# Expert tiles that wait for single chunks, slots filled from the front, and the first gathers moved into the experts' stage

## What is computed

```python
logits = xf @ Wg + bg
topv, topi = jax.lax.top_k(logits, K)              # K = 2
wts = jax.nn.softmax(topv, axis=-1)
order = jnp.argsort(-wts[:, 0])
...
cap = int(CAP_RATIO * T / E)                       # 1.25 * T / 8 = 15680
oneh = jax.nn.one_hot(tiF, E, dtype=jnp.int32)     # tiF: the picks in that order
pos = jnp.take_along_axis(jnp.cumsum(oneh, axis=0) - 1, tiF[:, None], axis=1)[:, 0]
keep = pos < cap
...
h = jax.nn.gelu(jnp.einsum('ecd,edf->ecf', eb, W1) + b1[:, None, :], approximate=False)
y = jnp.einsum('ecf,efd->ecd', h, W2) + b2[:, None, :]
contrib = yf[slot] * gate[:, None]
```

## Time and profile before

| | us |
|---|---|
| median of 3 runs | 6634.87 (6634.27 to 6637.27) |
| the profiled execution | 6633.88 |
| its span, first to last instruction | 6632.1 |

### The profile page before, as it was taken

The page is one execution under the profiler, slowest core; times in us unless marked ns, Lnnn a source line. Parts: engine busy times, 40 slices in busy tenths (PEclk is TensorE's granted clock), DMA queues, the critical chain, the costliest instruction groups (busy, mean ns, idle before and its releaser), DMA issues. The chain is left out here.

```text
span 6632.1 us, 69063 instructions
## 1 busy us (share of the span) xinstructions
PE 4831.6 (73%) x20564; PEld 2709.5 (41%) x20564; DVE 2371.6 (36%) x4527; ACT 1459.2 (22%) x3608; POOL 3834.9 (58%) x3737
## 2 busy tenths in 40 slices
PE   9999996102777979877987783466776677777778
PEld 4555666101444444434544441233333333333334
DVE  0012248970222222212222222444445545444442
ACT  2233344500222323222332230000000010000001
POOL 0000000008887888778877825777777777777770
PEclk9999998555888989888998896688888888888889
DMA  8877779812333333232333223222222222222210
GB/s 170 185 185 196 192 201 275 286 56 65 100 98 103 108 97 89 86 86 85 101 89 87 74 58 106 81 87 91 89 88 76 70 72 71 93 76 76 76 39 29
DMA packets 840381, 711.46 MB, mean 107 GB/s; under 512 B 596030, under 2 KB 681668, under 8 KB 836048
## 3 DMA queue, kind: packets, MB, share of 16 engines
q1 hardware_dynamic: 666320, 466.30, 25.8%
q0 software_dynamic: 109312, 139.69, 7.8%
q10 hardware_dynamic: 64512, 102.79, 4.5%
HBM read 440.11 MB, written 385.75 MB: 125 GB/s over the span
## 5 line engine op out<-in xcount | busy, mean ns | idle before, releaser
L1077 POOL DMA_INDIRECT y_ring<-ye,index_o x1568 | 1675.3, 1068 | 539.9 <-issue 452.1
L758 POOL DMA_INDIRECT xe<-chunk,index x1568 | 1539.6, 982 | 477.4 <-issue 476.1
L1110 PE MATMUL cp<-padded,taps_o 128*128 128x448 f32 x4032 | 1623.5, 561 | 49.8 <-DVE padded L1296 49.8
L1110 PEld LDWEIGHTS cp<-padded,taps_o 128*128 128x128 f32 x4032 | 785.5, 198 | 816.2 <-issue 795.6
L887 ACT ACTIVATE hid<-hid_ps,b_cols 128x448 f32<-128x448 f32 x1120 | 709.4, 633 | 1663.2 <-PE hid_ps L841 1565.1
L849 PE MATMUL y_ps<-hid,w_sb 128*128 128x448 f32 x2240 | 918.5, 554 | 0.4 <-DVE yt L912 0.4
L841 PE MATMUL hid_ps<-xt,w_sb 128*128 128x448 f32 x2240 | 890.9, 541 | 1.5 <-DVE xt L906 1.5
L1241 DVE SCALAR_TENSOR_TENSOR z<-y_ring,gates,z 128x128 f32<-128x128 f32 x1568 | 432.0, 347 | 905.0 <-DMA y_ring<-ye,index_o 890.1
L470 POOL MEMSET zeros<- 98x512 f32 x1 | 0.5, 524 | 1109.7 <-POOLq L105 1109.7
L1174 ACT ACTIVATE outb<-cp,shift,s 128x448 f32<-128x448 f32 x224 | 162.1, 723 | 2175.0 <-PE cp L1110 2175.0
L906 DVE COPY xt<-xt_ps 128x448 f32<-128x448 f32 x280 | 174.9, 625 | 1280.8 <-PE xt_ps L832 1278.2
(11 more groups left out here) (190 smaller groups left out, 3862.1 us busy)
## 6 DMA issues: line engine op xcount, KB each, us to landing
xe<-zeros SPq DMA_DIRECT2D x16, 3920.0 KB
rows_in<-xe SPq DMA_DIRECT2D x280, 224.0 KB, 2.6
ye<-rows_out SPq DMA_DIRECT2D x280, 224.0 KB, 2.3
xin<-in_x_dram SPq DMA_DIRECT2D x256, 196.0 KB
conv<-rows ACTq DMA_DIRECT2D x256, 196.0 KB
pix<-conv SPq DMA_DIRECT2D x224, 224.0 KB, 5.1
xn<-hat SPq DMA_DIRECT2D x112, 448.0 KB, 4.4
chunk<-xn POOLq DMA_DIRECT2D x112, 448.0 KB, 3.9
```

What stands on the lines that cost most here:

```text
L758: pool.indirect_dma_start(out=xe[:, :], out_offset=bass.IndirectOffsetOnAxis(ap=index[ch][:, c, j:j + 1], axis=0), in_=chunk[ch][:, j * C: ...
L1077: pool.indirect_dma_start(out=y[ch][c][:, j * C:(j + 1) * C], out_offset=None, in_=ye[:, :], in_offset=bass.IndirectOffsetOnAxis(ap=index[ ...
L1110: last = pe.matmul(cp[i % 2][:, 0:HB * W], taps[:, t, :], padded[b][:, img, hb * HB + kh:hb * HB + kh + HB, kw:kw + W], start=(t == 0), st ...
```

## The change

- Slots fill from the front: `spare` is gone. A token's slot starts from its expert's first slot, and an expert with fewer rows than its capacity leaves its last slots empty.
- `needed` counts chunks (1 to 112), not pairs. It is worked out with one tile per partition and brought into a row by a small DMA of SP.
- POOL waits after each chunk until that chunk's own scatters have landed, and raises `chunks_scattered`. The waits for the scatters of earlier chunks go.
- `y_ring`, its semaphores and the index tiles are allocated outside the two last stages. When the scatter is done, POOL copies the indices and clears the ring's parts for the first 4 chunks (`PRE`), waits until the first 14 rounds of tiles are stored (no row of the first pair of images can lie behind them, as the slots fill from the front), and gathers the 4 chunks. The output stage starts with the fifth.
- SP also writes zeros over each expert's slots 6272 to 15679 of `ye` (8 transfers), in the route stage.
- The convolution's weights pass through `summed[1]` in place of the last part of `y_ring`; its first load of x waits until they are read.
- The bound of the indirect DMAs' indices is put into a register once per stage instead of being given as a number with each DMA.

```diff
+PRE = 4
@@ route_phase
+    LATE = 2 * HW
+    ZL = (CAP - LATE) // ZP
...
+            for e in range(E):
+                sp.dma_start(ye[e * CAP + LATE:(e + 1) * CAP, :].rearrange("(p a r) c -> p a (r c)", p=ZP, r=4),
+                             zeros[:].unsqueeze(1).to_broadcast([ZP, ZL // 4, 4 * C])).then_inc(zeroed, 16)
+            sp.wait_ge(needed_set, 1)
+            sp.dma_start(needed[0:1, :, :], needed_by_tile[0:TILES, :]).then_inc(needed_out, 16)
+            sp.wait_ge(needed_out, 16)
+            sp.wait_ge(zeroed, 16 * (ZD + E))
...
+            pe.matmul(sums[:, 0, 0:1], below[:], tile_rows[:], start=True, stop=True).then_inc(tiles_counted, 1)
...
+            do(dve.tensor_tensor(tile_end[:], sums[:, 0, 0:1], tile_rows[:], ALU.add))
...
             scan_flags(work[:], 1)
-            do(dve.tensor_scalar(spare[:], run[:, :, GR - 1], -1.0, float(CAP), ALU.mult, ALU.add))
-            do(dve.tensor_tensor(run, run, spare[:].unsqueeze(2).to_broadcast([128, E, GR]), ALU.add))
-            do(dve.tensor_tensor(spare[:], spare[:], expert_base[:], ALU.add))
-            do(dve.tensor_tensor(base, base, spare[:].unsqueeze(2).to_broadcast([128, E, GR]), ALU.add))
+            do(dve.tensor_tensor(base, base, expert_base[:].unsqueeze(2).to_broadcast([128, E, GR]), ALU.add))
+            do(dve.tensor_scalar(short[:], run[:, :, 0:GR - 1], tile_end[:, 0:1], None, ALU.is_lt))
+            do(dve.tensor_reduce(fewer[:], short[:], AX_X, ALU.add))
+            dve.tensor_scalar(needed_by_tile[:], fewer[:], 1.0, None, ALU.add).then_inc(needed_set, 1)
             do(dve.tensor_tensor(groups_flat(tokens_flat(prio)), before_token, over_tokens(base), ALU.add))
-            do(dve.tensor_tensor_scan(tile_end[:], one_row[:, 0:1].to_broadcast([128, TILES]),
-                                      tile_rows[:, 0:1].to_broadcast([128, TILES]), 0.0, ALU.mult, ALU.add))
-            by_pair = run.rearrange("p e (g c) -> p e g c", c=NCHK)[:, :, 0:PR - 1, NCHK - 1]
-            do(dve.tensor_tensor(short[:], by_pair.unsqueeze(1).to_broadcast([128, TILES, E, PR - 1]),
-                                 tile_end[:].unsqueeze(2).unsqueeze(3).to_broadcast([128, TILES, E, PR - 1]), ALU.is_lt))
-            do(dve.tensor_reduce(fewer[:], short[:], AX_X, ALU.add))
-            do(dve.tensor_scalar(needed[:], fewer[:], 1.0, None, ALU.add))
@@ expert_phase
+    FIRST_PAIR = 2 * HW // NT
...
+            limit = pool.to_reg(DROP - 1)
...
-                    if not (first and ch < 2):
-                        pool.wait_ge(scattered[ahead], ahead_pair * PER_PAIR)
-                    if not first or ch == NCHK - 1:
-                        pool.wait_ge(scattered[(ch + 1) % NCHK], (g + (ch + 1) // NCHK) * PER_PAIR)
...
-                                bounds_check=DROP - 1, oob_is_err=False).then_inc(scattered[ch], 16)
+                                bounds_check=limit, oob_is_err=False).then_inc(scattered[ch], 16)
                     rest(n)
-                    if ch == 0 and not first:
-                        for c in range(NCHK):
-                            pool.wait_ge(scattered[c], g * PER_PAIR)
-                        pool.sem_inc(pairs_scattered, 1)
+                    pool.wait_ge(scattered[ch], (g + 1) * PER_PAIR)
+                    pool.sem_inc(chunks_scattered, 1)
...
+            for ch in range(PRE):
+                pool.tensor_tensor(index_o[ch][:], slots[:, :, ch * CHK:(ch + 1) * CHK],
+                                   zero[:].unsqueeze(2).to_broadcast([128, 2, CHK]), ALU.add).then_inc(index_set, 1)
+                pool.memset(y_ring[:, ch * 2 * CC:(ch + 1) * 2 * CC], 0.0).then_inc(index_set, 1)
+            pool.wait_ge(index_set, PR * NCHK + 1 + 2 * PRE)
+            for i in range(RING):
+                pool.wait_ge(tile_out[i], 16 * FIRST_PAIR * E // RING)
+            for ch in range(PRE):
+                for j in range(CHK):
+                    for c in range(2):
+                        pool.indirect_dma_start(
+                            out=y_ring[:, (ch * 2 + c) * CC + j * C:(ch * 2 + c) * CC + (j + 1) * C], out_offset=None, in_=ye[:, :],
...
-                sp.wait_ge(pairs_scattered, sp.value_load(needed[0:1, bass.ds(q, 1), e:e + 1].rearrange("p q e -> p (q e)"),
-                                                          min_val=1, max_val=PR))
+                sp.wait_ge(chunks_scattered, sp.value_load(needed[0:1, bass.ds(q, 1), e:e + 1].rearrange("p q e -> p (q e)"),
+                                                           min_val=1, max_val=PR * NCHK))
@@ output_phase
-        wc_rows = y_ring[:, (NCHK - 1) * 2 * CC:(NCHK - 1) * 2 * CC + C * 9]
+        wc_rows = summed[1][:, 0:C * 9]
...
             load_x(0, 0)
+            sp.wait_ge(const_turned, 10)
             load_x(1, 1)
...
-            set_index(0, 0)
+            set_index(PRE, PRE)
             def pair(g, first):
-                for ch in range(NCHK):
+                for ch in range(PRE if first else 0, NCHK):
```

More of the change, by code:

```diff
@@ L394, in _, with route_phase @@
                 chunk(m)
-def route_phase(nc, s, logits, xe, slots, gates, needed):
+def route_phase(nc, s, logits, xe, ye, slots, gates, needed):
     PR, J, CAP, DROP, TILES = s["PR"], s["J"], s["CAP"], s["DROP"], s["TILES"]
@@ L406, in route_phase @@
     ZP, ZR, ZD = 98, 80, 16
-    assert ZP * ZR * ZD == E * CAP
+    LATE = 2 * HW
+    ZL = (CAP - LATE) // ZP
+    assert ZP * ZR * ZD == E * CAP and ZP * ZL == CAP - LATE and ZL % 4 == 0
     GR = PR * NCHK
@@ L428, in route_phase @@
         taken = junk
-        expert_base, spare = sb("expert_base", [128, E]), sb("spare", [128, E])
-        tile_rows, tile_end = sb("tile_rows", [128, 1]), sb("tile_end", [128, TILES])
-        short, fewer = sb("short", [128, TILES, E, PR - 1], BF16), sb("fewer", [128, TILES, E])
+        expert_base = sb("expert_base", [128, E])
+        tile_rows, tile_end = sb("tile_rows", [128, 1]), sb("tile_end", [128, 1])
+        short, fewer, needed_by_tile = sb("short", [128, E, GR - 1], BF16), sb("fewer", [128, E]), sb("needed_by_tile", [128, E], U32)
         total = ctx.enter_context(nc.psum_tensor("total", [128, GROUPS, 512], F32))
@@ L654, in _, with expert_phase @@
                 do(dve.tensor_scalar(slots[:, c, 0:J], rel[:], float(DROP), None, ALU.add))
-def expert_phase(nc, s, xn, xe, ye, slots, needed, ln_beta, W1, b1, W2, b2, layer_scale):
+def expert_phase(nc, s, xn, xe, ye, slots, needed, index_o, y_ring, y_in, ln_beta, W1, b1, W2, b2, layer_scale):
     PR, DROP, TM, CAP, TILES = s["PR"], s["DROP"], s["TM"], s["CAP"], s["TILES"]
@@ L667, in expert_phase @@
     PER_PAIR = 2 * CHK * 16
+    FIRST_PAIR = 2 * HW // NT
+    assert FIRST_PAIR * NT == 2 * HW and RING == E
     with ExitStack() as ctx:
@@ L936, in _, with output_phase @@
             result(end - 1, E - 1, TILES - 1, False)
-def output_phase(nc, s, x, xn, ye, ln_beta, slots, gates, out, p):
+def output_phase(nc, s, x, xn, ye, ln_beta, slots, gates, index, y_ring, y_in, out, p):
     PR, N = s["PR"], s["N"]
@@ L968, in output_phase @@
         cleared = sem("cleared")
-        index = [sb(f"index_o{c}", [128, 2, CHK], U32) for c in range(NCHK)]
-        y_ring = sb("y_ring", [128, NCHK * 2 * CC])
         y = [[y_ring[:, (c * 2 + i) * CC:(c * 2 + i + 1) * CC] for i in range(2)] for c in range(NCHK)]
-        wc_rows = y_ring[:, (NCHK - 1) * 2 * CC:(NCHK - 1) * 2 * CC + C * 9]
         z = [sb(f"z{c}", [128, CC]) for c in range(NCHK)]
         summed = [sb(f"summed{b}", [C, 2 * HW]) for b in range(2)]
+        wc_rows = summed[1][:, 0:C * 9]
         padded = [sb(f"padded{b}", [C, 2, H + 2, PW]) for b in range(2)]
@@ L989, in output_phase @@
         index_set = sem("index_o_set")
-        y_in = [sem(f"y_in{c}") for c in range(NCHK)]
         xn_in = [sem(f"xn_in{c}") for c in range(NCHK)]
@@ L1052, in _ @@
             pool.wait_ge(zero_set, 1)
+            limit = pool.to_reg(s["DROP"] - 1)
             def set_index(n, slot):
@@ L1070, in pair @@
                     set_index(n + 1, (ch + 1) % NCHK)
-                    if first and ch == NCHK - 1:
-                        pool.wait_ge(const_turned, 10)
                     pool.memset(y_ring[:, ch * 2 * CC:(ch + 1) * 2 * CC], 0.0).then_inc(cleared, 1)
-                    pool.wait_ge(cleared, n + 1)
+                    pool.wait_ge(cleared, n + 1 - PRE)
                     for j in range(CHK):
@@ L1314, in build @@
             conv_norm_phase(nc, s, x, dw_kernel, dw_bias, bands, conv, xn, ln_gamma, ln_beta, Wg, bg, logits)
-            route_phase(nc, s, logits, xe, slots, gates, needed)
-        expert_phase(nc, s, xn, xe, ye, slots, needed, ln_beta, W1, b1, W2, b2, layer_scale)
+            route_phase(nc, s, logits, xe, ye, slots, gates, needed)
+        index_o = [ctx.enter_context(nc.sbuf_tensor(f"index_o{c}", [128, 2, CHK], U32)) for c in range(NCHK)]
+        y_ring = ctx.enter_context(nc.sbuf_tensor("y_ring", [128, NCHK * 2 * CHK * C], F32))
```

(4 more changed lines are left out.)

14 lines of the change are left out of this document (7 added, 7 removed).

## The result

The changed kernel takes 8209.15 us (median of 4 runs, 8206.95 to 8260.25); the kernel before, on the same chip, 6634.57 (6632.76 to 6637.27). The ratio is 1.239, 95% interval 1.234 to 1.244: slower by 1575 us. The forecast was 8249, with a range from 8210 to 8290. The profiled execution took 8208.58 us, its span is 8206.8.

The account below looks back on a forecast made before the run. POOL's indirect DMAs, 1.28 and 1.30 us apart, were taken to pace the experts' and output stages. Span 6632.1 + 6.9 + 1692.9 - 82.8 - 3.2 = 8245.9; with time outside the span 8249, range 8210 to 8290.

Parts of the forecast that it names:

- setup to the first gather: Output stage, from POOL's first instruction at 4023.64 to its first gather: the 14.9 us stay, change 0.
- behind the last gather: End of the output stage: the 148.1 us behind the last gather stay, change 0.
- Tiles behind the scatter: Experts' stage: 268 tiles instead of 21 stand behind the last scatter; 247 more at 6.854 us, +1692.9 us.
- the rival in which it wouldn't: Tile burst behind the scatter: TensorE's clock drops to 0.83 of full speed, adding 376 us, 8625; 2 in 100.
- Even experts: Rival, experts' stage: every expert fills its capacity, only some 8 tiles need the last chunk, near 6478; 2 in 100.
- chunks as the cause: Experts' stage, count by chunks: tile 0 goes after 4 chunks rather than 8, but nobody gains, as tile 4 is next.
- The new wait of POOL, once a chunk: Scatter: POOL waits for each chunk's 14 scatters to land; 0 to 25 us in all, taken as 0.
- The zeros: Route stage: 38.5 MB more zeros at 286 GB/s set its end; the experts' stage starts at 1478.6, +6.9 us.
- The bound in a register: Indirect DMAs: one 29 ns MOVE less each, counting only behind the output stage's memsets, 0.03 x 108 = -3.2 us.
- MOVEs in series: Rival, scatter and output stage: every removed MOVE saves its time, 8249 - 86 = 8163; 4 in 100.
- Early gathers: Four chunks' 56 gathers leave the output stage, hidden under the tile stream from about 4554 to 4640: -82.8 us.
- The rival in which the output stage takes the 82.8 us back: Output stage keeps its length, through the first pair's readers or a lost phase: 8332; 3 in 100.

Follow-up runs that it names:

- The first experiment: Kernel before with slots filled from the front, still pairs, no register, early gathers or ye zeros: 8329.74 us, ratio 1.199 where the kernel before takes 6946.91.
- the four kernels on the second: Kernel before with: all bounds in register, 6633.41 us; output-stage bounds except each chunk's first, 6754.23; ye zeros alone, 6768.83; those zeros in two transfers each, 6771.7.

## Why the prediction came out as it did

The forecast's sum against the two traces, term by term (us; after minus before):

| term | forecast | measured |
| --- | --- | --- |
| experts' stage starts later | +6.9 | +14.8 |
| from there to the held load (scatter, new wait) | 0 | +0.2 |
| held load to output stage | +1692.9 | +1691.7 |
| setup to the first gather | 0 | -0.6 |
| four chunks gathered early | -82.8 | -82.8 |
| gathers from the fifth chunk to the last | -3.2 | -49.7 |
| behind the last gather | 0 | +1.1 |
| sum, span | +1613.8 | +1574.7 |

The row of the four chunks is no test of its own: both of its values are the time that they took in the kernel before, and the row below it starts at that kernel's fifth chunk. Without the MOVEs the four take 80.8 us (third chip, above).

*Tiles behind the scatter.* Right, in mechanism and size. Chunk 87 and chunk 112 were named as the holders of tiles 4 and 12, for about 3335 and 3868; the loads came at 3346.7 and 3876.4, later by the 8 us of the zeros and, for the first, some 4 more. SP's two long waits, 1703 us and about 491, are the forecast's 1700 and 500. 268 tiles at 6.85 us followed, at a clock of 0.98 where the earlier trace rows have 1.00, so the burst's pace held for a stretch seven times as long, and the rival in which it wouldn't is out. The step that mattered was to ask which expert is the shortest and where its last row stands, not how many rows are in all.

*Even experts, and chunks as the cause.* The first experiment has the same 1693 us more behind the held load with pairs; the count by chunk neither causes nor cures it. Where the slots are at the end, it helps.

*The new wait of POOL, once a chunk.* Taken as 0, measured 0: both kernels scatter at 21.30 us a chunk. The held load went out 2.19 us after the last scatter's start, inside the 3.59 us that the rest of a chunk gives as cover. The Trainium skill's fit (DMA: Bandwidth & Descriptors, "Anatomy of one DMA — SWDGE (gpsimd) path") gave an estimate of 2.15 us for this. The trace of the kernel after agrees: it shows the scatters' landings, which that of the kernel before doesn't, 2.1 to 2.2 us for the last 14 and 2.2 us in the middle of them all:

```profile
L759 POOL DMA_INDIRECT xe<-chunk,index x1568: 975/980/1052, 1493.7 to 3874.2; - x196
...
DMA to landing us min/median/max: 2.1/2.2/6.6
```

*The zeros.* Named rightly as the new end of the route stage, at a pace that was too good. I had carried the 286 GB/s of the first buffer's zeros over to the second's. The end of the route stage, SP in time and its wait:

```profile
1293.26 27.95 SPq L468 DMA_DIRECT2D xe<-zeros  x2
1321.27 139.13 SPq L471 DMA_DIRECT2D ye<-zeros  x8
1460.45 6.92 SPq L474 DMA_DIRECT2D needed<-needed_by_tile  x1
```
```profile
SPq L476 <- DMA ye<-zeros: 18.7, 1, 18.7
```

Until 1336 it is 287 GB/s, but from 1360 on 268 to 278, and the wait ends at 1486.0. VectorE ended at 1457.8, 3 us before the forecast, and is worth nothing, as said. The mis-sized term is 8 us; zeros alone reproduce it, so the copy isn't the reason, and cutting the transfers in two doesn't mend it. Why the pace falls is open.

*The bound in a register.* This is the step that failed: -3.2 us in the sum, -49.7 measured. The 46.5 us between them are more than the whole 40 us of the forecast's error; the zeros, wrong by 8 us the other way, gave part of it back. It also carried the result out of the range, whose bounds allowed the MOVEs 40 us at most. The forecast saw the gap of 0.79 us behind the memset in the earlier trace rows and the ordinary one of 0.30, and put only the MOVE's own 29 ns of that down to the MOVE; the path that it had wrong is that the gather's issue waits behind the MOVE. The question to ask of the 0.49 us between them was what else the sequencer had to do after the memset, and the earlier trace rows had the answer beside it, 14 MOVEs in 6.9 us: 0.53 us a gather. At 0.5 us for 108 chunks the term would have been -54 us and the sum 8198, 11 us from the result, 8 of them the zeros'. One MOVE, left in just that place, keeps the loss whole. The rival "MOVEs in series" is out: it would have given 43.8 us in the output stage by 1512 MOVEs, close to the 49.7 measured, but also 45.5 in the scatter, whose length didn't move, and the pitch inside a chunk stayed at 1.31 us. Same size, another mechanism; the gap's place tells them apart.

*Early gathers.* Forecast from about 4554 to 4640, found here:

```profile
L782 POOL DMA_INDIRECT y_ring<-ye,index_o x56: 1000/1004/1057, 4587.9 to 4659.9; - x56
```

Some 34 us late: 8 are the zeros', and for the rest I had counted 100 tile pitches from the held load, but not the way of the last tile from its load to its store (3876.4 + 685.4 is 4561.8, and the store was issued at 4584.7). It was wholly hidden on this chip. The rival in which the output stage takes the 82.8 us back is out: its first gathers go out at the pace of the later ones. That they are free is not so on every chip: on the third the output stage starts 61 us later for them, which leaves 14.9 us of gain. My sum had a single pace for TensorE and no price for POOL beside it, since the earlier trace rows showed none; that holds for the chip I read it on.

## What to carry to other kernels

When one engine serves work in a fixed order and each piece waits for its own data, find the piece whose data is complete last and see where it stands in the order; a change of layout that looks neutral can put it first. A finer wait is worth only what stands behind the last one. And when a gap behind a wait is longer than the engine's usual one, count everything that is issued after the waiting instruction, not only that instruction's own time.

## What the runs showed of the hardware that I had not expected

A MOVE of 29 ns that takes over a semaphore wait ahead of a POOL indirect DMA costs 0.50 us each time that the wait really ends late (56.1 us over 112). The 1456 other MOVEs of the output stage cost nothing (2389.4 us of gathers without any, 2448.8 with only the 112 in front of first gathers, 2445.7 with all).

The kernel before takes 6634, 6758, 6947 and 6634 us on the first, second, third and last chip; the changed one 8209 on the first, 8272 on the third and 8207 on the last. Each chip's runs are of one time, so chip and time aren't told apart. The difference lies in the tile stream while POOL's indirect DMAs go out beside it: of the tile results, 1 came more than 7.2 us after the last (gaps under 20 us) in the kernel before on the first chip, 151 to 173 in the four kernels on the second. (On the last chip it is 1 in the kernel before again, and 25 in the one with single chunks and slots at the end, where tiles also wait for their chunks.) The second chip's kernel with the first bound as a number, from 1700 to 4120 us, shows where:

```profile
ACT hid L887 <- remote: 613.8, 128, 11.9
...
DVE xt L906 <- remote: 584.4, 92, 10.8
```
```profile
2301.53 0.62 DVE L906 COPY xt<-xt_ps 128x448 f32<-128x448 f32 x1 [6.12 <-remote]
...
2307.83 0.74 DVE L912 TENSOR_SCALAR yt<-y_ps,b_cols,scale_col 128x448 f32<-128x448 f32 x1 [5.67 <-remote]
2307.92 2.21 ACT L887 ACTIVATE hid<-hid_ps,b_cols 128x448 f32<-128x448 f32 x4 [8.02 <-remote]
```

In the same stretch of time TensorE had ended the last transpose into xt_ps at 2297.9 and the last matmul into y_ps at 2300.9; VectorE began to read them at 2301.5 and 2307.8, 3.7 and 6.9 us later, with nothing of its own in between. The kernel before on the first chip has no such line in that stretch. Where POOL is idle, behind the scatter, the pace is 6.85 us on every chip. The late starts also have a place in POOL's chunk of 21.3 us, counted from the same trace: of VectorE's 139 "remote" waits over 3 us in the scatter, 80 end within 3 us of the start of POOL's memset, the pause behind its 14 scatters, and of ScalarE's 49, 43 do; none ends in the 10 us after that. The two rows at 2307.8 and 2307.9 lie in such a pause, from 2305.67. So my reading is that on some chips, or at some times, the signals from TensorE reach the other engines late while POOL issues indirect DMAs, and that what has been held up comes through when it pauses. The ends of matmuls are modelled in the profile, and no experiment changed POOL's pauses on a chip that shows this; why it happens stays open. It would also explain why the changed kernel differs so little between chips: it has hardly a tile beside its scatters.
